# Graph kernel: neighbour lists without one self edge, in chunks of 3, all tiles at once, and row tiles in the adjacency build

## The reference, cut to what matters

```
h = relu(layernorm(x));  x = x + gin3(h)      # 3 layers
    gin layer: agg = segment_sum(h[src] * edge_weight, dst);  h = relu((agg + h) @ w1 + b1) @ w2 + b2
h = relu(layernorm(x));  x = x + gat3(h)      # 3 layers
    src, dst = concat(src, arange(n)), concat(dst, arange(n))     # one more self edge each
    emb = sin/cos embedding of node_vec, two linear maps;  x = h @ init_w + emb
    gat layer: xw = x @ W (8 heads);  logit = leaky_relu(al_s[src] + al_d[dst])
               e = exp(logit - segment_max(logit));  alpha = e / segment_sum(e)
               out = segment_sum(alpha * xw[src]);  x = silu(batchnorm(out + x @ adj_w + b))
```

## Time and profile before

| what | value |
|---|---|
| median of 3 runs | 5514.25 us |
| the profiled execution | 5531.82 us |
| its span | 5530.3 us |
| mean granted TensorE clock | 0.676 |
| POOL busy | 2781.9 us, 50% |
| PE busy | 2609.5 us, 47% |
| DVE busy | 2382.5 us, 43% |
| ACT busy | 595.1 us, 11% |

### The profile page before, as it was taken

One profiled execution on the slowest core, in us unless ns is written; L12 is line 12 of the kernel. 1 busy time (PEld: TensorE's weight loads), 2 busy tenths in 40 slices (PEclk: granted clock), 3 DMA queues, 4 the chain that ended last, 5 costly groups with the idle time before them and its releaser, 6 DMA issues. The chain is left out here.

```text
span 5530.3 us, 62828 instructions
## 1 busy us (share of the span) xinstructions
PE 2609.5 (47%) x13804; PEld 1907.7 (34%) x13804; DVE 2382.5 (43%) x7342; ACT 595.1 (11%) x1968; POOL 2781.9 (50%) x2942
## 2 busy tenths in 40 slices
PE   1666774354545445446355444445543333333333
PEld 1555542123333333334233333333432332332323
DVE  5888513324444444442444444444423333333333
ACT  2222300110000000003000000000020000000001
POOL 2000011356666666663566666666446666666663
PEclk9777887667677766778767677777765555555555
DMA  2222563033333333332333333333312221222222
GB/s 61 106 103 90 242 218 156 26 81 88 89 89 89 89 90 88 91 88 46 81 91 88 89 89 88 88 88 90 67 34 45 47 47 45 47 46 46 46 47 21
DMA packets 246618, 451.19 MB, mean 82 GB/s; under 512 B 163452, under 2 KB 165314, under 8 KB 241709
## 3 DMA queue, kind: packets, MB, share of 16 engines
q0 software_dynamic: 122928, 318.15, 23.6%
q1 hardware_dynamic: 111150, 128.71, 6.9%
q10 hardware_dynamic: 12384, 2.25, 0.3%
HBM read 392.07 MB, written 57.21 MB: 81 GB/s over the span
## 5 line engine op out<-in xcount | busy, mean ns | idle before, releaser
L495 POOL DMA_INDIRECT rows_all<-gat_tab,ell x2664 | 2517.2, 945 | 1566.2 <-issue 799.4
L1003 PE MATMUL banks<-rows_all,ident 128*128 128x264 f32 (+1 forms) x5328 | 1795.9, 506 | 2272.9 <-PEq L119 1791.5
L1003 PEld LDWEIGHTS banks<-rows_all,ident 128*128 128x128 f32 x5328 | 1305.8, 286 | 2763.1 <-issue 2576.9
L1575 DVE COPY lrel<-m_all 128x8 f32 x666 | 133.9, 201 | 1536.2 <-issue 1201.8
L1600 DVE TENSOR_TENSOR rows_all<-rows_all,banks 128x1024 f32<-128x1024 f32 (+1 forms) x666 | 685.7, 1042 | 218.8 <-issue 142.7
L789 ACT ACTIVATE banks<-ex_in 128x40 f32<-128x40 f32 x666 | 138.3, 208 | 3771.3 <-ACTq L119 2499.9
L1553 DVE TENSOR_TENSOR acc<-acc,banks 128x264 f32 (+1 forms) x675 | 259.7, 385 | 469.3 <-DVEq L119 278.1
L1546 DVE TENSOR_TENSOR acc<-acc,banks 128x264 f32 (+1 forms) x675 | 258.0, 382 | 107.0 <-issue 102.3
L859 PE MATMUL banks<-rows_all 128*128 128x52 bf16 x4992 | 187.5, 202 | 157.0 <-PEq L119 151.6
L495 POOL DMA_INDIRECT edges<-sw_d,edge_pick x28 | 34.6, 1236 | 412.5 <-POOLq L119 400.5
L859 PEld LDWEIGHTS banks<-rows_all 128*128 128x128 bf16 x4992 | 176.9, 108 | 182.3 <-issue 181.6
(11 more groups left out here) (276 smaller groups left out, 1974.2 us busy)
## 6 DMA issues: line engine op xcount, KB each, us to landing
rows_all<-gat_tab,ell POOLq DMA_INDIRECT x2664
x_t<-adj_d SPq DMA_DIRECT2D x11, 3328.0 KB
y_t<-adj_d SPq DMA_DIRECT2D x11, 3328.0 KB
adj_d<-x_t SPq DMA_DIRECT2D x7, 3328.0 KB, 10.0
adj_d<-y_t SPq DMA_DIRECT2D x6, 3328.0 KB, 9.8
ell<-ell_d SPq DMA_DIRECT2D x666, 2.5 KB
acc<-key_d SPq DMA_DIRECT2D x1, 1664.0 KB, 6.4
acc<-vec_d SPq DMA_DIRECT2D x1, 1664.0 KB, 18.6
```

The source lines that it names most:

```text
L495: return g.indirect_dma_start(out=dst, out_offset=None, in_=table, in_offset=bass.IndirectOffsetOnAxis(ap=idx, axis=0))
L1003: last = t.matmul(sum_ps[u % SUMS][:, 0:width], ident[:, :], rows[u][:, r * width:(r + 1) * width], start=(r == 0), stop=(r == SLOTS - 1))
```

## The change

1. **One self edge leaves the lists.** `weigh_all` finds which nodes have a self edge among their first 63 (`has_self`), sorts by the degree without it (`deg_net`) and puts it into the record (REC 4 to 5). `list_steps` moves the sources behind it one slot forward. In the attention layers `keep_rows` starts a tile's sums with (1 + has_self) times the node's own row, where it started with the row once.
2. **Chunks of 3 by rounds of 8.** SLOTS 4 to 3, RING 6 to 8, SUMS 3 to 4; a list block is 63 edges, 21 chunks. Padding slots of partition p name row PAD + p of the table instead of one row for all. SP loads the list entries of four chunks with one DMA (`ell_load`), and a buffer of four is freed once.
3. **Lists for all tiles at once.** POOL gathers all 26 tiles' edges before the reduction (`edges_all`), and again 26 by rank for the lists; VectorE makes all lists in wide operations, spread over pairs 10 to 12 of the first stage and pair 0 of the next; POOL then stores 26 tiles. ScalarE ranks all 26 tiles, in the build. The tile-by-tile loop remains behind `if more > 0`.
4. **Row tiles in the build.** The low one-hot has 26 columns. PE multiplies the upper and the lower 64 partitions apart, as two row tiles, into two banks: 16 x 3 x 2 matmuls of 26 columns per group. The build's pairs are written out one after the other instead of looping.

The core of the diff:

```diff
-SLOTS = 4
-PER_BLOCK = BLOCK // SLOTS
+SLOTS = 3
+LIST = 63
+PER_LIST = LIST // SLOTS
-RING = 6
+RING = 8
+LOAD = RING // 2
-SUMS = 3
+SUMS = 4
-PART_W = GROUP_DST * PAIR * T
+PART_W = GROUP_DST * T
+HALF_ROWS = P // PAIR
...
@@ sync: list entries @@
-                    for u in range(RING):
+                    for h in range(RING // LOAD):
                         take(sp, ell_free)
-                        sp.dma_start(ell[u][:, :], ell_d[:, bass.ds(it * RING + u, 1), :].rearrange("p k c -> p (k c)"))\
-                          .then_inc(ell_landed[u], 16)
+                        sp.dma_start(ell_load[h][:, :, :], ell_d[:, bass.ds(it * RING + h * LOAD, LOAD), :]).then_inc(ell_landed[h], 16)
...
@@ gpsimd @@
+            take(pool, pick_ready)
+            for t in range(T):
+                gather(pair_all[:, t, :, :].rearrange("p s c -> p (s c)"), sw_d, pick_all[:, t:t + 1]).then_inc(pair_gathered, 16)
+            take(pool, ell_ready)
+            for t in range(T):
+                start = pool.value_load(start_i[0:1, t:t + 1], min_val=0, max_val=CHUNKS - PER_LIST)
+                g.dma_start(ell_d[:, bass.ds(chunks_from(start), PER_LIST), :], ell_all[:, t, :, :]).then_inc(ell_stored, 16)
+                pool.wait_ge(ell_stored, (t + 1) * 16)
...
                     for u in range(RING):
-                        take(pool, ell_landed[u], 16)
-                        pool.sem_inc(tile_known, 1)
+                        if u % LOAD == 0:
+                            take(pool, ell_landed[u // LOAD], 16)
+                            pool.sem_inc(tile_known, LOAD)
                         take(pool, rows_free)
...
@@ tensor: part @@
                     for k in range(WEIGHT_PARTS):
-                        last = t.matmul(part_ps[n][:, q, :], hi_hot[n][:, q, :], lo_w[n][k][:, q, :], start=(k == 0), stop=(k == WEIGHT_PARTS - 1))
+                        for j in range(PAIR):
+                            rows_j = slice(j * HALF_ROWS, (j + 1) * HALF_ROWS)
+                            last = t.matmul(part_ps[n][:, j, q, :], hi_hot[n][rows_j, q, :], lo_w[n][k][rows_j, q, :],
+                                            start=(k == 0), stop=(k == WEIGHT_PARTS - 1), tile_position=(j * HALF_ROWS, 0))
...
@@ vector: masks and self edges of all tiles, after the first pair's one-hots @@
+            def weigh_all():
+                inside = link.mark(v.tensor_tensor(in_list, slot_f[:, :].unsqueeze(1).to_broadcast([P, T, BLOCK]), per_tile(deg), ALU.is_lt))
+                hit = link.mark(v.tensor_tensor(self_hit, edges_all[:, 0:T, :, 0], per_tile(id_f[:, :]), ALU.is_equal))
+                link.mark(v.tensor_tensor(edges_all[:, rest, :, 1], edges_all[:, rest, :, 1], in_list[:, rest, :], ALU.mult))
+                link(v.tensor_tensor(self_hit, self_hit, in_list, ALU.mult))
+                signal(edge_w_ready)
+                link(v.tensor_reduce(has_self[:, :], self_hit[:, :, 0:LIST], AX.X, ALU.max))
+                link(v.tensor_tensor(deg_net[:, :], deg, has_self[:, :], ALU.subtract))
...
@@ vector: lists @@
+                link(v.tensor_tensor(list_hit, source, per_tile(recs[:, :, 2]), ALU.is_equal))
+                link(v.tensor_tensor_scan(flat_list(list_seen), flat_list(list_later), flat_list(list_hit), 0.0, ALU.mult, ALU.max))
+                yield
+                link(v.tensor_tensor(list_move, after, source, ALU.subtract))
+                link(v.tensor_tensor(list_move, list_move, list_seen, ALU.mult))
+                yield
+                link(v.tensor_tensor(list_move, list_move, source, ALU.add))
+                link(v.tensor_tensor(list_hit, slot_f[:, 0:LIST].unsqueeze(1).to_broadcast([P, T, LIST]), per_tile(recs[:, :, 1]), ALU.is_lt))
+                yield
+                link(v.scalar_tensor_tensor(list_move, list_move, pad_at[:, 0:1], list_hit, ALU.subtract, ALU.mult))
+                link(v.tensor_scalar(ell_all[:, :, :, 0:SLOTS], list_move.rearrange("p t (k r) -> p t k r", r=SLOTS), pad_at[:, 0:1], None, ALU.add))
+                signal(ell_ready)
...
@@ vector: end of weigh(u) @@
-                        signal(ell_free)
+                        if u % LOAD == LOAD - 1:
+                            signal(ell_free)
```

More of the change, by code:

```diff
@@ new lines, in _, with chunks_from @@
+            take(pool, pick_ready)
+            for t in range(T):
+                gather(pair_all[:, t, :, :].rearrange("p s c -> p (s c)"), sw_d, pick_all[:, t:t + 1]).then_inc(pair_gathered, 16)
+            def chunks_from(start):
+                return nc.s_assert_within(start, 0, CHUNKS - PER_LIST,
+                                          skip_runtime_bounds_check_because="CHUNKS has room for every tile's last block")
+            take(pool, ell_ready)
+            for t in range(T):
+                start = pool.value_load(start_i[0:1, t:t + 1], min_val=0, max_val=CHUNKS - PER_LIST)
+                g.dma_start(ell_d[:, bass.ds(chunks_from(start), PER_LIST), :], ell_all[:, t, :, :]).then_inc(ell_stored, 16)
+                pool.wait_ge(ell_stored, (t + 1) * 16)
@@ L717, in keep_pair @@
                         keep_mid(0)
+                    if k >= 2 and c in RANKS_AFTER:
+                        for tile in itertools.islice(ranked, 1):
+                            rank_of(tile)
             act.wait_ge(weights_landed, 16 * WEIGHTS)
-            keep_pair(0, first=True)
-            with act.Fori(0, PAIRS // 2):
-                for u in (1, 0):
-                    keep_pair(u)
+            for k in range(PAIRS):
+                if k == 2:
+                    act.wait_ge(key_landed, 16)
+                keep_pair(k)
+            act.sem_inc(keys_counted, 1)
             keep_agg(0)
             keep_mid(0)
-            act.wait_ge(key_landed, 16)
-            ranked = iter(range(DVE_TILES, T))
             for l in (1, 2):
@@ L1275, in one_hot @@
                 for k in range(WEIGHT_PARTS):
[L1276 removed]
+                    last = v.tensor_tensor(pairs(lo_w[n][k]), pairs(lo_hot[n]), each(w_two[u][k], T), ALU.mult)
                 last.then_inc(hot_ready[n], 1)
@@ L1301, in build_pair @@
                     one_hot(u, c)
-                if not first:
+                if first:
+                    weigh_all()
+                else:
                     keep_hidden(k - 1, h_mid)
```

407 lines of the change are left out of this document (210 added, 197 removed).

## The result

The changed kernel takes 5742 us (median of 4 runs, 5723 to 5765) against 5516 for the kernel before in the same measurement: ratio 1.041, interval 1.039 to 1.043. The forecast was 5279; the time lies outside its range and on the other side. The profiled execution of the changed kernel has a span of 5721.5 us against 5530.3, +191.

A forecast was written before the change was run, and what follows sets the result against it. It took the chunks handed back per run of gathers, not bytes, to bound the loops; build 0, lists -90 and loops -145 sum to -235 from 5514, so 5279 us, range 5110 to 5470.

The forecast's parts named there:

- Their new price: Attention gather loops: each of 2520 gathers costs 1.565 us, ends 1.47 and 1.63, so the loops change by -145 us.
- rival C: Gather loops: POOL waits for half-buffer list loads behind its wait for rows; +151 us, 5665 in all; chance 0.08.
- Gathers removed: Attention loops: one self edge less and chunks of 3 give 840 gathers a layer for 888; -221 us at today's price.
- The lists: GIN stages ahead of the loops: making all tiles' lists at once gives -90 us, ends -40 and -120.
- The build: Build ahead of the GIN stages: start 30 us later, pairs of 33 us for 35, sum 0; ends -85 and +165.
- The prediction's other end: Build, slow end of its range: 43 ns per matmul makes a pair 47 us, +165 us.
- A: Gather loops: smaller chunks return fewer rows, nine gathers per run; loops +19 us, 5443 in all; chance 0.17.
- B: Loops or build: fifteen gathers per run (-300 us) or overlapping row tiles (build -85), say 5170 us; chance 0.19.
- D: Second GIN stage: stores and gathers slow PE, so the lists gain nothing; 5349 us; chance 0.53 together with the forecast.

## Why the prediction was wrong, by its own steps

**Their new price: the step that failed.** The forecast was 1.565 per gather, bounded at 1.63; it is 1.71, 358 us more over the loops. I took the number of chunks returned per run as the only bound, from runs in which a list buffer was always free before the rows, and put the half loads at nothing. That was the failing term: with loads of two, all else as changed, a gather costs 1.541, a little under the 1.565 forecast. The mechanism stood in the prediction as rival C with a chance of 0.08. Its sum for the loops came close (462 us of exposed loads against some 392 by the trace, and 362 to 423 by the loops with loads of two), partly by luck: it had 3.3 us on two thirds of 210 halves. Shown is a wait on one half per round, 102 of them; POOL stands 6.3 us at it, of which 3.8 are beyond the time when its rows are free. They are the load's 2 and, ahead of it, what VectorE's order puts between PE's sum and the end of weigh 3. I had written that the fourth weighing comes just after the sum that frees the rows. It does take that sum, but what frees the rows is PE's own end of it, 2.4 us before the half was free in the timeline above (4821.7 and 4824.1). What I had set against C, that the start of a run often leaves a load time, was so in none of the 102 rounds. And it falls on the round's start alone, where VectorE has just spent a whole run of gathers at its loop top and POOL is as far ahead as it can be. Changing LOAD from 4 to 2 alone gives 6.4% in one series (5687 to 5321 us), and moves the kernel from 4.7% slower to 2.2% faster than the kernel before.

**Gathers removed.** 2520 as counted. But chunks of 3 at 1.541 with the shorter gate cost what chunks of 4 at 1.492 do: in the same series the saving of 72 gathers brought nothing.

**The lists.** -90 forecast. Stage two gained more than forecast for its pairs and less for its tail: 13 pairs in 135 us for 232, and 20 us from the last result to x_res for 27, together -104 against -96. Stage one was mis-sized: the scatters stopped the first pair for 38 us, not the 20 less 14 that I took, so what stands between the last one-hot and the first pair's result grew from 39 to 60 us. Together with the start and the build all came to -57.

**The build.** +27 for the reduction (30 forecast), and 35.7 us a pair for 33. The bound of TensorE was right in kind and wrong in working: the matmuls overlap (12.5 ns, not 25), and gaps in TensorE's stream stand in their place. That VectorE's 26 would be reached without them is not shown: with a third of the matmuls a pair still took 29.2. The prediction's other end, 43 ns at the slow clock, did not come either: runs without a gap take 12.8 ns a matmul on the mean at a granted clock of 1.00 and 13.6 at 0.50. The rule of about 60 cycles of overhead per matmul (the Trainium skill, "TensorEngine Tiling (Array Packing)", Instruction Overhead), which I had half believed, does not hold at the slow clock even for each tile by itself: by it two tiles that overlap would start 25 ns apart, and 13.6 is measured. At the fast clock 12.5 is just what it would give.

**Sums of the prediction.** Its 4089 us of loops are lengths of windows; from first to last gather they are 4073, so 1.529 per gather and not 1.535. A pair of 50 us in the build would have given +204 by the sum that it uses elsewhere, not +180. Neither changes the outcome.

**Rivals A, B and D.** Nine per run was rare; runs were mostly of 15 to 21 and then 3 or 6. The lists gained. The overlap of B is real and gains nothing.

## What to carry to other kernels

When a buffer's refill is made coarser, write down in the consumer's order which step frees it and which step frees the resource that bound so far: a half load cost nothing where the two fell together (three chunks of 4), and some 4 us a round where it came two steps later (four chunks of 3). Fewer instructions on the busiest engine do not help while it waits for others, and a part that makes chunks smaller adds steps on exactly those. A measurement on one chip may show a wait that another does not have at all.

## What the runs showed of the hardware

In a long run of indirect gathers or scatters on GpSimd, 1.25 us apart, other engines' instructions are slow to start. From TensorE's timeline in the first GIN stage of the changed kernel, during the record scatters:

```profile
643.99 0.59 PE L889 MATMUL banks<-y_t,h_mid 128*64 128x256 f32 x1 [0.73 <-issue]
645.39 1.01 PE L889 MATMUL banks<-y_t,h_mid 128*64 128x256 f32 x2 [0.82 <-issue]
```

Matmuls that start 0.1 us apart ahead of this come one or two at a time, with 0.7 to 0.8 us of idle time between and nothing to wait for. VectorE's register steps take 0.7 us in place of 0.02 to 0.3. In the loops of both kernels the first slow step of a run comes 8 to 12 us behind its first gather (medians of the layers) and the last ends up to some 4 us behind the end of its last. A rest of 1.4 us per chunk of four keeps it off entirely; 0.76 us leaves 126 to 157 slow steps a layer for 188 to 247 and 0.44 us leaves 162 to 201. Two of the chips (kernel before 4760 and 4763 us) never show it in the loops, and the kernel before is 12 to 14% faster there. An estimate from its 2664 gathers at a plain 1.25 us, 3330 us for the 4073 of its loops, is about as much. What it is I can't say.

Matmuls on two row tiles of 64 x 26 columns start 12.5 ns apart, where whole-array ones of 52 columns started 25 ns apart; at a granted clock of 0.50 it is 13.6 and 43.

Gaps of 0.5 to 3.9 us inside TensorE's runs of matmuls end 1.2 to 1.6 us behind the end of a packet of the instruction queue, in every trace of this build that I counted (the kernel before, the changed one, chunks of 4, one weight part, no row tiles).
